# A graph layer on one core: h turned by VectorE in squares of 32 and moved by ScalarE, with another first unit

## The reference

```python
h = jnp.maximum(_layernorm(x, axis=-1), 0.0)
deg = jnp.sum(adj, axis=1, keepdims=True) + 1e-05
adj_norm = adj / deg
h_neigh = adj_norm @ h
out = h_neigh @ W_neigh.T + b_neigh + h @ W_self.T + b_self
result = x + jax.nn.relu(out)
```

## Time and profile before

| what | us |
|---|---|
| median of 3 runs | 433.58 (433.25 to 434.57) |
| the profiled execution | 431.64 |
| its span | 429.8 |
| TensorE busy | 417.0 |
| VectorE busy | 372.9 |
| ScalarE busy | 208.8 |
| GpSimd busy | 135.0 |

### The profile page before, as it was taken

How to read it: one execution, slowest core, us unless ns; L and a number is a source line. 1 busy time by engine, 2 the same in 40 slices (tenths; PEclk the granted TensorE clock), 3 DMA queues, 4 the chain that set the end, 5 groups by cost and what they waited for, 6 DMA issues and landing times.

```text
span 429.8 us, 5641 instructions
## 1 busy us (share of the span) xinstructions
PE 417.0 (97%) x2034; PEld 353.1 (82%) x2034; DVE 372.9 (87%) x466; ACT 208.8 (49%) x267; POOL 135.0 (31%) x107
## 2 busy tenths in 40 slices
PE   9999999999999599998999999999999999999995
PEld 8888888888887488887988888888888888888884
DVE  6899989999970799799989989999979797979954
ACT  5786576655330733346147337436342643426411
POOL 2777677389402505012403403203010302003021
PEclk9999999999999699999999999999999999999999
DMA  8989999885696695535535645445645365453101
GB/s 299 379 283 327 292 321 294 235 238 197 204 257 132 162 277 192 185 111 212 180 106 202 216 135 196 162 159 187 205 147 195 129 226 185 146 197 146 49 2 49
DMA packets 25339, 83.99 MB, mean 195 GB/s; under 512 B 2784, under 2 KB 4320, under 8 KB 25312
## 3 DMA queue, kind: packets, MB, share of 16 engines
q1 hardware_dynamic: 22864, 75.77, 50.9%
q0 software_dynamic: 2016, 7.34, 9.0%
q10 hardware_dynamic: 432, 0.52, 0.4%
HBM read 79.43 MB, written 4.19 MB: 195 GB/s over the span
## 4 chain that ended last, share of the span: by engine, by line
PE 87%; issue 6%; DVE 5%; ACT 2%; DVEq 0%; ACTq 0%
PE banks L659 66%; PE banks L718 10%; DVE total L469 2%; PE banks L767 2%; PE banks L677 1%; PE banks L675 1%; PE banks L676 1%; PE banks L709 1%; PE banks L636 1%; ACT h_row L306 1%; ACT adj_hi L303 1%; DVE own L538 1%; PE banks L760 0%; PE banks L691 0%; PE banks L692 0%
## 5 line engine op out<-in xcount | busy, mean ns | idle before, releaser
L303 ACT ACTIVATE adj_hi<-adj_raw 128x1024 fp32r<-128x1024 f32 x127 | 133.8, 1058 | 140.3 <-PE banks L659 137.7
L457 DVE TENSOR_TENSOR adj_lo<-adj_raw,adj_hi 128x1024 fp32r<-128x1024 f32 x127 | 170.5, 1344 | 17.0 <-ACT adj_hi L303 17.0
L659 PE MATMUL banks<-adj_lo,h_hi 128*128 128x512 f32 x472 | 127.2, 391 | 4.7 <-DVE adj_lo L457 4.7
L469 DVE TENSOR_TENSOR total<-total,adj_raw 128x1024 f32<-128x1024 f32 x106 | 128.6, 1214 | 0.0
L659 PE MATMUL banks<-adj_hi,h_hi 128*128 128x512 f32 x472 | 128.5, 394 | 0.0
L659 PE MATMUL banks<-adj_hi,h_lo 128*128 128x512 f32 x472 | 126.2, 389 | 0.0
L659 PEld LDWEIGHTS banks<-adj_lo,h_hi 128*128 128x128 f32 x472 | 89.0, 189 | 23.5 <-DVE adj_lo L457 5.1
L659 PEld LDWEIGHTS banks<-adj_hi,h_lo 128*128 128x128 f32 x472 | 88.6, 188 | 18.7
L659 PEld LDWEIGHTS banks<-adj_hi,h_hi 128*128 128x128 f32 x472 | 87.1, 189 | 16.5
L258 POOL TENSOR_TENSOR own<-own,b_sum 128x1024 f32<-128x1024 f32 x8 | 28.1, 3518 | 102.3 <-ACT own L352 102.3
L264 POOL TENSOR_TENSOR x_sb<-x_sb,own 128x1024 f32<-128x1024 f32 x7 | 23.0, 3290 | 116.1 <-ACT own L367 116.1
(11 more groups left out here) (87 smaller groups left out, 378.2 us busy)
## 6 DMA issues: line engine op xcount, KB each, us to landing
adj_raw<-adj_in SPq DMA_DIRECT2D x128, 512.0 KB, 3.3
total_dma<-adj_in POOLq DMA_DIRECT2D x14, 512.0 KB, 7.6
x_sb<-x_in SPq DMA_DIRECT2D x14, 256.0 KB, 7.1
rows_out<-x_sb SPq DMA_DIRECT2D x7, 512.0 KB, 2.6
rows_out<-x_sb SPq DMA_DIRECT2D x3, 128.0 KB, 1.8
x_sb<-x_in ACTq DMA_DIRECT2D x1, 256.0 KB, 6.4
own<-w_neigh SPq DMA_DIRECT2D x1, 256.0 KB, 5.7
own<-w_self SPq DMA_DIRECT2D x1, 256.0 KB, 5.6
```

Source lines behind the costliest of these rows:

```text
L303: nc.scalar.activation(adj_hi[:, s % RING, :, :], adj_raw[:, s % RAW, :, :], ACT.Copy).then_inc(s_hi, 1)
L457: nc.vector.tensor_tensor(adj_lo[:, r, :, :], adj_raw[:, s % RAW, :, :], adj_hi[:, r, :, :].bitcast(F32), ALU.subtract).then_inc(s_lo, 1)
L469: nc.vector.tensor_tensor(total[:, q % 2, :, :], total[:, q % 2, :, :], adj_raw[:, s % RAW, :, :], ALU.add).then_inc(s_add, 1)
L659: done = nc.tensor.matmul(banks[:, MAIN[q % 2][k], :], m[:, j, k * P:(k + 1) * P], part[:, r, a, :], start=(j == 0 and stage == 0), stop=F ...
```

## The change

h is no longer made again and turned on TensorE. `turn`, `make_h_again`, `turned_high`, `turned_low` and `ident` go. VectorE turns the high and the low part of the block's h, which are still there from the start, with four transposes of 128x512 a block; VectorE's transpose turns each 32x32 square in its place (`turn_squares`, at `square_at[q]` = `own_at[q]` - 5 and the unit after it). ScalarE then moves the squares to their partition quarters, in 16 instructions a block of 32 partitions and 512 elements each, four after each of four units' splits (`move_squares`), into `ht`. The squares lie in `shared`, which also holds what was h_row, own and total_dma: the high parts in h_row's place, the low parts in own's place for block 0 and in the second half of total_dma for the others. So `turn_squares` of block 1's low part waits until the DMA sums are joined.

The first unit is no longer split: TensorE multiplies h in fp32 by the loaded adj in fp32, four matmuls, after nine warm-ups of 512 columns instead of 34 of 128. The unit is loaded in two halves. VectorE's steps at the start come in another order. `make_fold` moves to the start of GpSimd's program. The adding DMAs of block 1 may start at TensorE's units 23, 26, ... 36 instead of 28, 30, ... 43. Several tables of unit numbers move by a few units.

The core of the diff:

```diff
-WARM = 34
+WARM = 9
...
-    dma_from = [5, 8, 11, 15, 18, 22, 25, 28, 30, 33, 35, 38, 40, 43]
+    dma_from = [5, 8, 11, 15, 18, 22, 25, 23, 26, 28, 30, 32, 34, 36]
...
-    turn_at = [32, 44, 58, 68, 78] + [16 * q + 8 for q in range(5, Q)]
-    own_at = [36, 48, 61, 71, 81] + [16 * q + 11 for q in range(5, Q)]
+    own_at = [36, 50, 60, 69] + [16 * q + 11 for q in range(4, Q)]
...
+    square_at = [o - 5 for o in own_at]
...
-    halves_at = [(32, 35), (50, 51)]
+    halves_at = [(32, 35), (43, 44)]
...
+            def move_squares(q, a):
+                act.wait_ge(s_square, 4 * q + 4)
+                if q >= 1:
+                    act.wait_ge(s_own, 2 * q)
+                low = 1 if q == 0 else 3
+                rows = slice(32 * a, 32 * a + 32)
+                for b in range(4):
+                    feats = slice(32 * b, 32 * b + 32)
+                    last = nc.scalar.activation(
+                        ht[feats, :, :, :, rows].rearrange("p l t k r -> p l (t k) r"),
+                        shared[rows, 0:low + 1:low, :].rearrange("p l (n f) -> p l n f", f=P)[:, :, :, feats], ACT.Copy)
+                last.then_inc(s_ht, 1)
...
+            def turn_squares(q, part):
...
+                for n in range(2):
+                    tiles = slice(q * UI + 2 * n, q * UI + 2 * n + 2)
+                    nc.vector.transpose(shared[:, place, n * 2 * F:(n + 1) * 2 * F],
+                                        source[:, tiles, :].bitcast(F32).rearrange("p t f -> p (t f)")).then_inc(s_square, 1)
...
+            split_h(0)
+            first_offsets(slice(2, 4), 3)
             split_unit(1)
-            first_offsets(slice(2, 4), 3)
             pair_statistics(2)
+            split_unit(2)
             split_h(1)
-            split_unit(2)
...
+                    pe.wait_ge(*((s_raw0, 16) if a == 0 else (s_raw[0], 16)))
+                    pe.wait_ge(s_h0, a + 1)
+                    for k in range(KC):
+                        done = nc.tensor.matmul(banks[:, MAIN[0][k], :], h_row[:, 0, a, k * P:(k + 1) * P],
+                                                adj_raw[:, 0, a, :], start=(a == 0), stop=False)
...
-                nc.tensor.matmul(banks[:, SMALL[0], 0:P], p_hi[:, 0, 0:P], p_hi[:, 0, 0:P], start=True, stop=True)
+                nc.tensor.matmul(banks[:, SMALL[0], :], p_hi[:, 0, 0:P], p_hi[:, 0, :], start=True, stop=True)
```

More of the change, by code:

```diff
@@ L83, in gnn_layer @@
         p_lo = sb("p_lo", [P, KC, R], F32R)
-        ht_hi = sb("ht_hi", [P, KC, R], F32R)
-        ht_lo = sb("ht_lo", [P, KC, R], F32R)
-        own = sb("own", [P, UI, F])
+        ht = sb("ht", [P, 2, UI, KC, P], F32R)
         total = sb("total", [P, 2, UJ, R])
-        total_dma = sb("total_dma", [P, 2, UJ, R])
         sums = sb("sums", [P, 2, R])
@@ L170, in gnn_layer @@
         SMALL = [4, 5]
-        TURNED = [6, 7]
         SUMMED = 7
@@ L198, in _ @@
             sp.dma_start(x_sb[:, 0, :], x[:, 0, :]).then_inc(s_x[0], 16)
-            for s in range(S):
+            sp.dma_start(adj_raw[:, 0, 0, :], adj[0, 0, :, 0, :]).then_inc(s_raw0, 16)
+            sp.dma_start(adj_raw[:, 0, 1, :], adj[0, 0, :, 1, :]).then_inc(s_raw[0], 16)
+            for s in range(1, S):
                 load_unit(s)
@@ L506, in sum_runs @@
                   .then_inc(s_part, 1)
[L508 to L512 removed]
+            def turn_squares(q, part):
+                if part == 0:
+                    if q == 0:
+                        dve.wait_ge(s_hhi, PAIRS)
+                        dve.wait_ge(s_hlo, PAIRS)
+                    else:
+                        dve.wait_ge(s_ht, 4 * q)
+                elif q == 0:
+                    dve.wait_ge(s_wlo, 1)
+                elif q == 1:
+                    dve.wait_ge(s_both, 4)
+                source = (h_hi, h_lo)[part]
+                place = 0 if part == 0 else 1 if q == 0 else 3
+                for n in range(2):
+                    tiles = slice(q * UI + 2 * n, q * UI + 2 * n + 2)
+                    nc.vector.transpose(shared[:, place, n * 2 * F:(n + 1) * 2 * F],
+                                        source[:, tiles, :].bitcast(F32).rearrange("p t f -> p (t f)")).then_inc(s_square, 1)
             def product_low(q):
@@ L728, in own_product @@
                 for t in range(UI):
-                    last = small_product(banks[:, SMALL[t // 2], (t % 2) * F:(t % 2 + 1) * F], ht_hi, ht_lo, 1, t)
+                    for k in range(KC):
+                        for n, (part, w) in enumerate(((0, w_hi), (0, w_lo), (1, w_hi))):
+                            last = nc.tensor.matmul(banks[:, SMALL[t // 2], (t % 2) * F:(t % 2 + 1) * F], ht[:, part, t, k, :],
+                                                    w[:, k, 1, :], start=(k == 0 and n == 0), stop=(k == KC - 1 and n == 2))
                     if t % 2 == 1:
@@ L747, in weigh @@
                 for t in range(UI):
-                    last = small_product(banks[:, SMALL[t // 2], (t % 2) * F:(t % 2 + 1) * F], p_hi, p_lo, 0, t)
+                    cols = slice(t * P, (t + 1) * P)
+                    for k in range(KC):
+                        for n, (m, w) in enumerate(((p_hi, w_hi), (p_hi, w_lo), (p_lo, w_hi))):
+                            last = nc.tensor.matmul(banks[:, SMALL[t // 2], (t % 2) * F:(t % 2 + 1) * F], m[:, k, cols],
+                                                    w[:, k, 0, :], start=(k == 0 and n == 0), stop=(k == KC - 1 and n == 2))
                     if t % 2 == 1:
```

169 lines of the change are left out of this document (45 added, 124 removed).

## The result

The changed kernel takes 445.88 us (median of 4 runs, 445.60 to 447.36), the kernel before 434.07 us on the same chip (433.25 to 435.24). The ratio is 1.030, with a 95% interval of 1.027 to 1.033: slower by 3%. 416.5 us, faster, was predicted. In what follows the kernel before has medians from 429.9 to 434.1 us, so kernels are compared by their ratio to the kernel before on the same chip.

A forecast was written before the change was run, and what follows sets the result against it. TensorE's own sequence was taken as the bound. -8.3 - 7.0 - 1.1 - 2.2 + 1.5 = -17.1 us takes the median from 433.6 to 416.5 us; forecast's own range 412.5 to 419, overall 412.5 to 425.

The forecast's parts named there:

- (a): Middle, near 140 us: earlier make_fold and block 1 DMAs remove TensorE's stop and its slow clock; gain 8.3 us.
- R2: Rival: crowding costs 4 us and the start gains only 1.0, giving 420.2 us; chance 0.12.
- R1: Rival: adding DMAs land later, so the middle wait only moves and the slow clock returns; 424.8 us, chance 0.11.
- (b): All eight blocks: TensorE's transposes of h, 0.87 us each, leave the path; gain 7.0 us.
- (c): Block 2's own product: its wait for ht_lo goes; gain 1.1 us.
- (d): Start: fewer warm-ups and an unsplit fp32 first unit, 16 passes, ending near 10 us; gain about 2.2 us.
- (h): Start, GpSimd: make_fold's seven selects end near 3.5 us, before the first power is asked for.
- (e): VectorE: transposes replace low parts, about +1.4 us a block; 44 us against TensorE's 49.5, so it fits.
- (f): ScalarE: moves of 0.5 us, 2.9 us a unit; loses 0.8 us in all, covered by its 8 us lead.
- R3: Rival: quarter-crossing moves cost 1.06 us, TensorE stops every block; 452 us; decides from about 0.95 us; chance 0.05.
- (g): Crowded places, units 31 to 36 and 43 to 47: 1.5 us of stops, from 0 to 5.

The follow-up runs named there:

- The two edits alone: Kernel before with make_fold at the program's start and earlier due times for block 1's adding DMAs, nothing else: 425.16 us, ratio 0.984.
- later joins: Changed kernel with VectorE's two join_half of block 1 back at units 50 and 51, flip and reduce behind them: 444.03 us, ratio 1.034.
- short adds: Changed kernel with GpSimd's two adds of a block (bias and x) cut from 256 to 8 columns a tile, output incomplete: 434.07 us, ratio 1.013.
- one move: Changed kernel with ScalarE moving one of four squares of a row quarter from block 1 on, turned h incomplete: 423.48 us, ratio 0.980.
- spread moves: Changed kernel with two moves a unit over eight units, transposes ten units ahead, block 1's joins back, three units between products in blocks 2-4: 418.69 us, ratio 0.968.
- relu later: Changed kernel with relu of the block before, and its store, behind the moves on ScalarE instead of ahead of them: 445.26 us, ratio 1.030.
- short transposes: Changed kernel with VectorE's transposes from block 2 on cut to 32 columns each, turned h incomplete: 433.68 us, ratio 1.012.
- moves inside a quarter: Changed kernel with each ScalarE move writing the partition quarter it reads, so h isn't turned fully: 438.6 us, ratio 1.022.
- earlier transposes: Changed kernel with VectorE's four transposes of blocks 5 to 7 two units earlier: 448.1 us, ratio 1.035.

## Why the prediction was wrong

**(a) The stop in the middle: right for the parts, wrong for the whole.** The two edits alone gave 7.3 of 8.3 us. In the changed kernel a new stop of 6.9 us with its slow clock stands in the same block (columns: window, its length, busy us of PE, PEld, DVE, ACT and POOL with counts, granted clock, DMA share, GB/s):

```profile
148.00:152.00 4.00, 3.57 (x8) 2.81 (x9) 3.13 (x4) 3.92 (x6) 0.00 (x0) 0.50 0.54 186
```

It is nearer to R2 than to R1. The last adding DMA lands at 133.55, near the forecast 130, and VectorE waits 0.8 us for it. But the bias add before it holds VectorE for 2.2 us, and the joins, the transposes, the flip and the reduce then stand close together. It needed both cures, later joins and short adds: 7.6 us of stops with the adds cut alone, 2.8 and 3.9 with the later joins (four moves and one), 0.1 us with later joins, one move and short adds, and 0.3 with later joins, spread moves and short adds. R1, priced as a wait for the DMA alone, shows where VectorE is fast enough to be early. With relu later and the adds cut it waited 5.3 us:

```profile
DVE sums L459 <- DMA shared<-adj_in: 5.3, 1, 5.3
```

**(b) and (c) held.** TensorE's 64 transposes are gone. For the own product's wait of 1.1 us there are 0.7, for join_rows. The kernel with one move, later joins and short adds lands on 416.55 us, a ratio of 0.963 where the forecast is 416.5 / 433.6 = 0.961. That it is the same number is luck: this kernel also leaves out GpSimd's adds, which are worth 1% in the kernel before, and it loses 4.9 us ahead of block 0's own product. What it shows, and with all of the work the 0.968 of the spread moves too, is that most of the gain in the sum is there once the stops are gone.

**(d) and (h) held in size, gave less.** make_fold's seven selects take 2.90 us from 1.28 on and end at 4.18, not 3.5. The first unit's fp32 matmuls take 3.67 us and end at 11.03, where the first unit ended at 13.52 before:

```profile
7.36 3.67 PE L610 MATMUL banks<-adj_raw,shared 128*128 128x512 f32 x8 [1.69 <-ACT shared L301]
```

Each matmul has two records; their starts are 0.43 us apart and the whole over eight is 0.46, so 512 columns take 0.86 to 0.92 us, about four passes of 0.227. That is what the Trainium skill has (FP8 and Floating Point Precision, TensorE Precision Notes), and the forecast's 16 passes a unit. (The steps of (d) from 9.5 us add up to 14.5 to 15.1 us, not 14.3 to 14.9. Unit 2 ended near 16.4.) By block 0's own product 1.2 us of the 2.2 are left, and the whole times don't resolve them.

**(e) failed: right in size, wrong in effect.** VectorE is busy 45.9 us in a steady block, where the sum had 44. The transposes take 0.61 us each. But "it fits" looked at the average. The 2.2 us for which GpSimd's bias add holds VectorE were in no term, though the trace of the kernel before has them (GpSimd's add, VectorE's split beside it, and the group of all splits):

```profile
276.64 2.62 POOL L258 TENSOR_TENSOR own<-own,b_sum 128x1024 f32<-128x1024 f32 x1 [14.59 <-ACT own L352]
```
```profile
276.92 3.42 DVE L457 TENSOR_TENSOR adj_lo<-adj_raw,adj_hi 128x1024 fp32r<-128x1024 f32 x1
```
```profile
L457 DVE TENSOR_TENSOR adj_lo<-adj_raw,adj_hi 128x1024 fp32r<-128x1024 f32 x127 | 170.5, 1344 | 17.0 <-ACT adj_hi L303 17.0
```

With the adds cut the mean of that kernel's splits is 1216 ns. In the kernel before 11 of the 15 adds hold VectorE, 16 us in all, and ScalarE's lead hides most of it. In the changed kernel join_rows comes late by it, and what waits for join_rows is ScalarE. Cutting the transposes gave 1.8%.

**(f) is the step that failed.** It was wrong in three places. A move is 0.64 us instead of 0.5, so a unit is 3.66 us and four lose 3.8 us to TensorE, not 0.8. "Its lead of up to three units (8 us) covers it" was taken before the queue was followed: relu stands ahead of the first move and waits for join_rows, which stands behind the transposes and behind VectorE's delay, so ScalarE sat 5.45 us while its lead ran out. And of the end nothing was said: block 7's moves come right before TensorE's last units, and 4.7 us are lost there.

R3 had the right chain and the wrong threshold. It said that a move decides from 0.95 us on, with 5 us of lead left (its own terms give 0.89). Of the 3.8 us that four units lose to TensorE, 2.7 to 3.1 are stops in blocks 5 to 7, so about 1 us of lead was left at the first move, and 0.64 decided. R3 had a chance of 0.05.

**(g) failed with it:** 0 to 5 us of stops were allowed for two places, and 34 us were lost, 8.5 of them in blocks 5 to 7, which it didn't name at all.

What the runs don't add up to is a price for each. Of the kernel before's time one move saves 5.0%, short adds 1.7% (or 2.6%), short transposes 1.8%, relu later nothing, and relu later with short adds 4.7%. The 8.5 us of stops in blocks 5 to 7 show it best: 0.0 are left with one move, 0.5 with short adds, 2.5 with short transposes, 3.9 with moves inside a quarter, 5.9 with relu later, 7.9 with earlier transposes. Each cure works only as far as it gives the lead back. What share of block 2's and 3's stops belongs to VectorE's own crowding wasn't separated. The length of an add may count too: ScalarE waited 6.2 us for GpSimd's add of x before it copied block 4's own product. What that cost TensorE is open.

## What to carry to other kernels

A lead covers a burst only if it is still there when the burst begins: read what stands ahead of the moved work in its queue and what that waits for, and subtract. Work that an engine can do on average, but not in four units, is spread over eight. And before an average load is called a fit, look for rows of the same form that take two or three times the mean, and count what stands beside them.

## What the runs showed of the hardware

- A VectorE add or subtract of 128x1024 with both inputs in SBUF, behind a GpSimd add of 128x1024 that is under way, stops until that one ends, and then takes its own time. In four places it ended 1.07 to 1.09 us after GpSimd's: 321.05 after 319.97, 132.73 after 131.65, 366.67 after 365.58 (relu later), and 304.60 after 303.53 (spread moves). The Trainium skill says so (SBUF — State Buffer, Who interferes with whom: whichever starts first has the shared read interface for its whole instruction, and the other blocks). By that rule the price could be estimated before, with GpSimd's add of 2.67 us in the earlier trace rows: 15 adds on GpSimd, each up to 2.2 us on VectorE. The traces agree with it.
- GpSimd waits in its turn. In most places its add ends 2.2 to 2.3 us after the VectorE add or subtract that was at work when it was issued (354.24 after 351.98 in the changed kernel). In the changed kernel the add of x at 260.69 shows 7.88 us: five such VectorE instructions of 1.22 us each ran back to back beside it, and it ended 2.25 us after the last. So GpSimd didn't get in between them. That it can wait for five in a row isn't in the rule above.
- ScalarE's copies of 32 partitions by 512 elements start 0.64 us apart in a row when they cross a quarter and 0.52 to 0.54 when they don't. The 128x512 copies of the earlier trace rows are 0.49 apart.
